# Graph layer with max over seven relations: first batch reordered, row sums turned by VectorE and placed by GpSimd

## The reference

```
h   = relu(layernorm(x))
HW_r = h @ W[r, :128] + c_r          c_r = W_edges[r] @ W[r, 128:]   (one row of 128)
A_0 = A_1 = adj,  A_3 = A_4 = adj^T,  A_2, A_5: a shift over the batch axis or its transpose,  A_6 = identity
out = x + max over r of (A_r @ HW_r) + b
```

## Time and profile before

| | us |
|---|---|
| three runs: median (lowest, highest) | 230.85 (229.27, 233.23) |
| profiled execution: own time | 230.21 |
| its span | 228.5 |
| busy: TensorE / weight loads | 213.9 / 145.1 |
| busy: VectorE | 172.2 |
| busy: ScalarE | 159.0 |
| busy: GpSimd | 57.8 |

### The profile page before, as it was taken

How to read it: one execution, slowest core, us unless ns; L and a number is a source line. 1 busy time by engine, 2 the same in 40 slices (tenths; PEclk the granted TensorE clock), 3 DMA queues, 4 the chain that set the end, 5 groups by cost and what they waited for, 6 DMA issues and landing times.

```text
span 228.5 us, 3306 instructions
## 1 busy us (share of the span) xinstructions
PE 213.9 (94%) x872; PEld 145.1 (63%) x872; DVE 172.2 (75%) x414; ACT 159.0 (70%) x431; POOL 57.8 (25%) x109
## 2 busy tenths in 40 slices
PE   7973799999999899999999999999999998999994
PEld 7532466667676567667667667677666665667672
DVE  3453987697876887897779788797778869787845
ACT  3756928778686777969586877969686867966220
POOL 3106322303232231213223231213223231223200
PEclk9997589999999999999999999999999999999999
DMA  5999907759293955949393866939393966610101
GB/s 184 310 355 371 336 5 243 265 192 303 44 382 103 313 185 200 308 100 331 114 346 127 264 241 209 295 123 348 88 333 123 306 202 238 221 46 3 47 0 46
DMA packets 31586, 47.13 MB, mean 206 GB/s; under 512 B 1632, under 2 KB 11088, under 8 KB 31568
## 3 DMA queue, kind: packets, MB, share of 16 engines
q1 hardware_dynamic: 31568, 46.92, 61.4%
HBM read 42.72 MB, written 4.19 MB: 205 GB/s over the span
## 4 chain that ended last, share of the span: by engine, by line
PE 85%; SPq 5%; DMA 4%; DVE 2%; issue 2%; DVEq 0%
PE bank_g L691 12%; PE bank_p L736 12%; PE bank_gT L673 11%; PE bank_p L738 10%; PE bank_p L737 10%; DMA x_sb<-in_x_dram 4%; PE bank_p L714 3%; PE bank_g L695 3%; PE bank_gT L678 3%; PE bank_gT L679 3%; PE bank_g L696 3%; PE bank_g L699 3%; PE bank_gT L682 3%; PE bank_p L640 3%; PE bank_p L648 3%
## 5 line engine op out<-in xcount | busy, mean ns | idle before, releaser
L548 DVE TENSOR_TENSOR best<-bank_p,best 128x512 f32<-128x512 f32 x48 | 33.2, 692 | 9.1 <-PE bank_p L738 8.1
L295 POOL TENSOR_TENSOR x_bias<-xT_sb,bias_sb 128x512 f32<-128x512 f32 x16 | 20.7, 1294 | 73.7 <-DVE h_lo L517 72.1
L403 ACT ACTIVATE gT_hi<-bank_gT 128x512 fp32r<-128x512 f32 x16 | 9.6, 598 | 37.5 <-PE bank_gT L682 37.1
L691 PE MATMUL bank_g<-adjT_sb,h 128*128 128x512 f32 x60 | 29.0, 605 | 0.0
L545 DVE SCALAR_TENSOR_TENSOR best<-bank_p,c_col,best 128x512 f32<-128x512 f32 x32 | 24.0, 751 | 6.4 <-ACT best L422 5.7
L387 ACT ACTIVATE h<-x_sb,shift,rstd 128x128 f32<-128x128 f32 x60 | 24.7, 491 | 5.9 <-DVE shift L497 5.9
L673 PE MATMUL bank_gT<-adj_sb,h 128*128 128x512 f32 x60 | 28.2, 592 | 0.0
L303 POOL TENSOR_TENSOR o_sb<-best,x_bias 128x512 f32<-128x512 f32 x15 | 19.8, 1320 | 28.2 <-DVE best L548 28.2
L479 DVE BATCH_NORM_STATS2 stats<-x_sb 128x6 f32<-128x128 f32 x64 | 14.0, 281 | 16.4 <-DMA x_sb<-in_x_dram 16.4
L736 PE MATMUL bank_p<-hT_hi,w_hi 128*128 128x512 f32 x48 | 20.1, 419 | 4.0 <-issue 2.9
L511 DVE TENSOR_TENSOR aT_lo<-adjT_sb,aT_hi 128x512 fp32r<-128x512 f32 x30 | 21.8, 767 | 0.0
(11 more groups left out here) (107 smaller groups left out, 470.2 us busy)
## 6 DMA issues: line engine op xcount, KB each, us to landing
adj_sb<-in_adj_dram SPq DMA_DIRECT2D x15, 1024.0 KB, 5.4
adjT_sb<-in_adjT_dram SPq DMA_DIRECT2D x15, 1024.0 KB, 5.8
xT_sb<-in_xT_dram SPq DMA_DIRECT2D x16, 256.0 KB, 6.1
x_sb<-in_x_dram SPq DMA_DIRECT2D x15, 256.0 KB, 6.4
out_dram<-o_sb SPq DMA_DIRECT2D x15, 256.0 KB, 6.0
adj_sb<-in_adj_dram SPq DMA_DIRECT2D x4, 256.0 KB, 3.8
adjT_sb<-in_adjT_dram SPq DMA_DIRECT2D x4, 256.0 KB, 4.4
w_sb<-in_W_dram SPq DMA_DIRECT2D x3, 128.0 KB, 7.0
```

Source lines behind the costliest of these rows:

```text
L295: nc.gpsimd.tensor_tensor(x_bias[q][:, :], xT_sb[q][:, :], bias_sb[:, :], ALU.add).then_inc(xb_ready, 1)
L548: op = nc.vector.tensor_tensor(best[q][:, :], product, best[q][:, :], ALU.max)
L691: nc.tensor.matmul(bank_g[:, 0:N], h[q][:, c, :], adjT_sb[q][:, c, :], start=(c == WHOLE[0]), stop=False)
```

## The change

- x lies in four buffers instead of two (NX = 4); in the loop SyncE issues load_x(b + 3) where load_x(b + 2) stood.
- First loads: the weights of relations 2, 5, 6 and x(1) go out after the first chunk of adjT(0), the other weights ahead of adj(1), and x(2) after adjT(1).
- TensorE's turn_sums and ScalarE's copy_sumsT are gone. sum_parts shrinks to 32 columns for each chunk, of which 8 are used. VectorE turns it in 32x32 blocks (`turned`, row group = node group of 32); GpSimd's `place_sums` spreads it to sumsT of 128 x (4 chunks x 4 groups x 32 nodes), each row group keeping only its own nodes by the mask own_group.
- c_rows gets a plane of 128 rows for each of the four relations, and each c product is one matmul over all 128 rows (`add_sums`). c values come from four matmuls of 128 columns.
- In batch 0 VectorE's list is in another order, w_lo is made in three parts, and TensorE does products 0, 1, then the passes of 3 and 4, product 2, the passes of 5 and 6, and the four c products last (`products_first`).

```diff
@@ sync
-                q = b % 2
-                if b >= 2:
-                    sp.wait_ge(h_ready, b - 1)
+                q = b % NX
+                if b >= NX:
+                    sp.wait_ge(h_ready, b - NX + 1)
...
             for c in range(C):
                 sp.dma_start(adjT_sb[0][:, c, :], adjT_dram[0][:, c, :]).then_inc(adjT0_in[c], 16)
-                if c == 1:
+                if c == 0:
                     sp.dma_start(w_sb[:, 0:1, :], w_dram[:, 2:3, :]).then_inc(wh_in, 16)
                     sp.dma_start(w_sb[:, 1:3, :], w_dram[:, 5:7, :]).then_inc(wh_in, 16)
-            load_x(1)
-            load_adj(1)
+                    load_x(1)
             sp.dma_start(w_sb[:, 3:5, :], w_dram[:, 3:5, :]).then_inc(wa_in, 16)
             sp.dma_start(w_sb[:, 5:7, :], w_dram[:, 0:2, :]).then_inc(wa_in, 16)
+            load_adj(1)
             load_adjT(1)
+            load_x(2)
...
             for b in range(B):
+                if b + 3 < B:
+                    load_x(b + 3)
                 if b + 2 < B:
-                    load_x(b + 2)
                     load_adj(b + 2)
@@ gpsimd
+            def place_sums(b):
+                pool.wait_ge(sumsT_turned, b + 1)
+                if b == 0:
+                    pool.wait_ge(masks_ready, 1)
+                else:
+                    pool.wait_ge(prod_psum, b * NPROD)
+                nc.gpsimd.tensor_tensor(sumsT[:, :, :, :],
+                                        turned[:, :].rearrange("p (c s) -> p c s", c=C).unsqueeze(2)
+                                        .to_broadcast([P, C, C, GROUP]),
+                                        own_group[:, :].unsqueeze(1).unsqueeze(3).to_broadcast([P, C, C, GROUP]),
+                                        ALU.mult).then_inc(sumsT_ready, 1)
...
             part_sums(0)
+            nc.gpsimd.tensor_tensor(w_lo[:, NH + 2:, :], w_sb[:, NH + 2:, :], w_hi[:, NH + 2:, :].bitcast(F32),
+                                    ALU.subtract).then_inc(wlo_ready, 1)
+            place_sums(0)
...
                 part_sums(b)
                 finish(b - 1)
+                place_sums(b)
@@ vector
+            def turn_sums(b):
+                dve.wait_ge(parts_lo, b + 1)
+                if b >= 1:
+                    dve.wait_ge(sumsT_ready, b)
+                nc.vector.transpose(turned[:, :], sum_parts[b % 2][:, :, :].rearrange("p c k -> p (c k)").bitcast(F32)
+                                    ).then_inc(sumsT_turned, 1)
...
             scale_and_shift(1)
+            turn_sums(0)
+            dve.wait_ge(masks_ready, 1)
+            dve.wait_ge(c_step, 2)
+            for d in range(2):
+                rels = slice(2 * d, 2 * d + 2)
+                nc.vector.tensor_scalar(c_low[:, rels, :], c_rest[:, rels, :], row_lo[:, d:d + 1], None,
+                                        ALU.mult).then_inc(c_step, 1)
+                dve.wait_ge(c_step, 3 + d)
+                nc.vector.scalar_tensor_tensor(out=c_rows[:, rels, :], in0=c_hi[:, rels, :].bitcast(F32),
+                                               scalar=row_hi[:, d:d + 1], in1=c_low[:, rels, :], op0=ALU.mult,
+                                               op1=ALU.add).then_inc(crow_ready, 1)
+            split_g_lo(0)
+            take_best(0, 1)
+            split_h_lo(1)
             variance(2)
-            split_g_lo(0)
-            split_h_lo(1)
-            take_best(0, 1)
             take_best(0, 2)
...
                 if b + 1 < B:
                     scale_and_shift(b + 1)
+                turn_sums(b)
+                if b + 1 < B:
                     split_adj_lo(b + 1)
@@ tensor
-                nc.tensor.matmul(to[:, nodes], c_rows[rows, :], sumsT[rows, nodes], start=True, stop=False)
+            def add_sums(i, to, chunks=slice(0, C), start=False, stop=False):
+                return nc.tensor.matmul(to[:, chunks.start * P:chunks.stop * P], c_rows[:, ORDER_A.index(ORDER[i]), :],
+                                        sumsT[:, chunks, :, :].rearrange("k c g s -> k (c g s)"),
+                                        start=start, stop=stop)
+            def products_first():
+
+                product(0, 0)
+                product(0, 1)
+                pe.wait_ge(gTlo_ready, 1)
+                pe.wait_ge(wlo_ready, 2)
+                passes(3, bank_of[3][:, 0:N], start=True)
+                passes(4, bank_of[4][:, 0:N], start=True)
+                pe.wait_ge(ccol_ready, 1)
+                product(0, 2)
+                pe.wait_ge(c_step, 2)
+                pe.wait_ge(wlo_ready, 3)
+                pe.wait_ge(glo_ready, 1)
+                passes(5, bank_of[5][:, 0:N], start=True)
+                passes(6, bank_of[6][:, 0:N], start=True)
+                pe.wait_ge(crow_ready, 2)
+                pe.wait_ge(sumsT_ready, 1)
+                for i in range(NH, NPROD):
+                    add_sums(i, bank_of[i], stop=True).then_inc(prod_psum, 1)
...
             for b in range(1, B):
                 aggregate_T(b)
                 turn_h(b)
-                turn_sums(b)
                 aggregate(b)
```

More of the change, by code:

```diff
@@ L55, in sem @@
             return ctx.enter_context(nc.semaphore(name))
-        x_sb = pair("x_sb", [P, C, F])
+        x_sb = [sb(f"x_sb{i}", [P, C, F]) for i in range(NX)]
         xT_sb = pair("xT_sb", [P, N])
@@ L81, in gnn_kernel @@
         sums = pair("sums", [P, 2, C])
-        sum_parts = pair("sum_parts", [P, C, 2, 2, GROUP], F32R)
-        sumsT = sb("sumsT", [P, N], F32R)
+        sum_parts = pair("sum_parts", [P, C, GROUP], F32R)
+        turned = sb("turned", [P, C * GROUP])
+        sumsT = sb("sumsT", [P, C, C, GROUP], F32R)
         x_bias = pair("x_bias", [P, N])
@@ L106, in gnn_kernel @@
         e_blocks = sb("e_blocks", [R * REL, R])
-        e_rows = sb("e_rows", [R * REL, 4, GROUP])
+        e_rows = sb("e_rows", [R * REL, 4, P])
         bias_sb = sb("bias_sb", [P, N])
         c_col = sb("c_col", [P, R])
[L110 to L115, removed]
+        row_hi = sb("row_hi", [P, 2])
+        row_lo = sb("row_lo", [P, 2])
+        own_group = sb("own_group", [P, C])
+        c_hi = sb("c_hi", [P, 4, O], F32R)
+        c_rest = sb("c_rest", [P, 4, O])
+        c_low = sb("c_low", [P, 4, O])
+        c_rows = sb("c_rows", [P, 4, O], F32R)
         bank_gT = bank("bank_gT")
@@ L126, in gnn_kernel @@
         x0_in = [sem(f"x0_in{i}") for i in range(2)]
-        x_in = [sem(f"x_in{i}") for i in range(2)]
+        x_in = [sem(f"x_in{i}") for i in range(NX)]
         xT_in = [sem(f"xT_in{i}") for i in range(2)]
@@ L192, in times, with x_loads @@
             return 16 * ((b + 1) // 2)
+        def x_loads(b):
+            return 16 * (b // NX + int(b % NX > 0))
         def turns(b):
@@ L317, in _ @@
             for q in range(2):
-                last = nc.gpsimd.memset(sum_parts[q][:, :, :, :, :].bitcast(F32), 0.0)
+                last = nc.gpsimd.memset(sum_parts[q][:, :, :].bitcast(F32), 0.0)
             last.then_inc(parts_zeroed, 1)
@@ L448, in _ @@
             make_h(1)
-            copy_sumsT(0)
             act.wait_ge(ccol_ready, 1)
@@ L459, in _ @@
                 split_hT(b)
-                copy_sumsT(b)
                 if b + 1 < B:
@@ L477, in variance @@
                     elif b > 0 and c == 0:
-                        dve.wait_ge(x_in[q], times(b))
-                    last = nc.vector.bn_stats(stats[:, c, :], x_sb[q][:, c, :])
+                        dve.wait_ge(x_in[b % NX], x_loads(b))
+                    last = nc.vector.bn_stats(stats[:, c, :], x_sb[b % NX][:, c, :])
                 last.then_inc(stats_done, 1)
@@ L578, in _ @@
             dve.wait_ge(c_psum, 1)
-            nc.vector.tensor_copy(c_col[:, :], bank_c[:, 0:R]).then_inc(ccol_ready, 1)
-            nc.vector.tensor_copy(c_hi[:, :], bank_c[:, P:2 * P]).then_inc(c_step, 1)
+            c_psum_rows = bank_c[:, :].rearrange("p (r o) -> p r o", r=4)
+            nc.vector.tensor_copy(c_col[:, :], bank_ccol[:, 0:R]).then_inc(ccol_ready, 1)
+            nc.vector.tensor_copy(c_hi[:, :, :], c_psum_rows).then_inc(c_step, 1)
             dve.wait_ge(c_step, 1)
-            nc.vector.tensor_tensor(c_rest[:, :], bank_c[:, P:2 * P], c_hi[:, :].bitcast(F32),
+            nc.vector.tensor_tensor(c_rest[:, :, :], c_psum_rows, c_hi[:, :, :].bitcast(F32),
                                     ALU.subtract).then_inc(c_step, 1)
[L584 to L589, removed]
             variance(1)
@@ L641, in turn_h @@
                 last.then_inc(hT_psum, 1)
[L643 to L651, removed]
             def aggregate_T_first():
@@ L735, in product @@
                     hi, lo = g_hi, g_lo
-                nc.tensor.matmul(dst, w_hi[:, i, :], hi[:, nodes], start=(r in H_RELS), stop=False)
+                nc.tensor.matmul(dst, w_hi[:, i, :], hi[:, nodes], start=start, stop=False)
                 nc.tensor.matmul(dst, w_lo[:, i, :], hi[:, nodes], start=False, stop=False)
```

(27 more changed lines are left out.)

57 lines of the change are left out of this document (21 added, 36 removed).

## The result

| | median us (lowest, highest) | runs |
|---|---|---|
| before, beside it | 230.21 (229.27, 233.23) | 4 |
| after | 234.51 (233.64, 235.89) | 4 |

The ratio is 1.021, interval 1.013 to 1.028: the changed kernel is slower, but since 1.02 lies inside the interval, the runs do not settle whether it is slower by as much as 2%. The ratio leaves out the 233.23 of before, an execution in a slower state (1.7% above the fastest), and so differs a little from the quotient of the medians, 1.019. The profiled execution of the changed kernel took 235.89, its span 234.2; it is the slowest of its four.

The account below looks back on a forecast made before the run. TensorE bounds the kernel before; after the change VectorE's late hT_lo stalls it every batch. Batch 2 at 41.4, twelve batches of 13.65, batch 14 of 13.34 and a 16.5 tail give span 235.0, time 237; range 226 to 245.

Parts of the forecast that it names:

- The mechanism: VectorE's a_lo pair: GpSimd's placement runs between the two subtractions, delays hT_lo, and TensorE stalls in every batch.
- the hold: Blocking of VectorE's second a_lo subtraction by GpSimd's placement: +1.09 us a batch, bounds below 0 to above 2.6.
- period: Time per batch: hT_lo at +7.46, wanted at +6.64, product 0 at +7.56, plus 6.09: 13.65 us against a mean of 12.91.
- The c products: TensorE, each batch: four full passes at 0.234, 0.94, replace 0.62 of row-group passes and slower return: +0.31 us.
- The start: Up to batch 2: batch 1 begins 5.4 to 7.4 us earlier, about 2 survive; batch 2 at 41.4, before 43.46.
- a fall of the granted clock in the stalls: TensorE's clock could fall in stalls of 1 us; given nothing beyond the upper end of the range.
- Batch 14 and the tail: Batch 14, full collision without variance: 13.34 us; batch 15 and the tail, no stall: 16.5 against 16.86.
- The hidden placement: First rival: GpSimd served after both a_lo, beneath gT_lo and hT_lo; TensorE bounds at 12.47, time 220.6; chance 0.18.
- the second rival: Part of the hold hidden by shorter placement or escaping aT_lo pair: 0.3 to 0.8 off a period, 226 to 233; chance 0.15.
- The third: GpSimd slower on broadcast operands: 1.6 us instead of 1.28 gives 241.5, twice the time 255; chance 0.07.
- The x waits: VectorE's waits for x go with four buffers: up to -4.1 us; the rival that they stay shares the 0.07.

Follow-up runs that it names:

- The moved line: The changed kernel with VectorE's turn_sums after the two a_lo subtractions instead of before them: 221.66 us, ratio 0.966.
- the quarter: The changed kernel with GpSimd placing only one chunk of four from batch 1 on: one run of 224.14 us.
- the memset: The changed kernel with GpSimd's placement replaced from batch 1 on by a memset of the same tile: one run of 222.84 us.
- hT_lo first: The changed kernel with VectorE's list reordered: turn the sums, gT_lo, hT_lo, then the a_lo pair; 219.39 us, ratio 0.955.
- variance(3) late: The kernel with hT_lo ahead of the a_lo pair, and in batch 1 variance(3) after g_lo: 219.68 us, ratio 0.956.

## Why the prediction was right

It said 237 with the step slower, from a profiled execution of 236.7; the profiled one took 235.89 and the median is 234.51. Against the kernel before that is a loss of 4.3 us where 6.2 were forecast (237 for 230.85). The range of 226 to 245 would have held no change at all as well, so what the prediction is worth shows in its terms.

- **The mechanism held.** GpSimd got its turn between the two a_lo subtractions, TensorE was ready at +6.64 as counted, and TensorE stalled in every batch up to batch 14. The moved line, the quarter and the memset show that the hold, and not the work added, makes the loss.
- **The hold was sized too large:** 1.09 counted, 0.82 measured. The sum took over the hold that the o_sb addition makes, a GpSimd pass of 1.28 by itself; the placement, with both operands broadcast, takes 1.04 by itself. From the start of the transpose to the next instruction it is 0.23 (0.2 counted). hT_lo at +7.21 for +7.46, period 13.37 in the batch shown for 13.65; the twelve batches from 43.38 to 204.26 average 13.41, 2.9 us less than forecast in all.
- **The c products** came at +0.30 for +0.31. TensorEngine Tiling (Array Packing) in the Trainium skill (key properties) says that different tiles run in parallel, and also that a change of tiling mode drains TensorE. The prediction set only the first against the full passes; the rows fit both: four 32-row passes took 0.43 together, and the first full pass behind them 0.42 instead of 0.23.
- **The start** was right up to 28.2: batch 1 began at 23.45 in the timeline (23.4), the last maximum of batch 0 ended at 28.21 (28.6), and TensorE waited for it. Then one term failed: the prediction gave a fall of the granted clock in the stalls nothing beyond the upper end of the range, and counted all of batch 1 at full clock. TensorE stood 1.21 and 2.91 us, and its next passes ran at half clock. Timeline of TensorE after, and the stretch with its granted clock (columns as in the earlier trace rows):

```profile
34.60 0.76 PE L752 MATMUL bank_p<-hT_hi,w_hi 128*128 128x512 f32 x1 [2.91 <-issue]
35.17 0.63 PE L753 MATMUL bank_p<-hT_hi,w_lo 128*128 128x512 f32 x1
...
34.60:40.30 5.70, 5.70 (x14) 4.44 (x15) 2.34 (x4) 4.04 (x13) 1.99 (x5) 0.50 0.61 207
```

  Batch 2 began at 43.38 instead of 41.4. From product 0 on, 34.60 to 43.38 is 8.78 where a full clock needs 6.05: 2.7 us. Of the 7.2 gained in batch 0 (23.45 for 30.68 in the timelines) nothing was left. How much of this the other executions pay is not shown: their mean granted clock was 0.985 to 0.993 against 0.980 in the profiled one, and their spans were 1.4 to 2.3 us shorter.
- **Batch 14 and the tail.** Batch 14 took 13.07 for 13.34. The tail was to shrink by 0.37 and took 16.87, as before: the maxima began 0.38 earlier in it, and VectorE then waited 0.58 before the last one, where it had waited 0.20. Why is not shown. The full-height c passes are not the cause: put on the kernel before, they leave that wait at 0.20.
- **The errors offset, by luck:** -2.9 in the twelve batches and -0.3 in batch 14 against +2.0 at batch 2 and +0.4 in the tail leave the span at 234.2 for 235.0. A good total is not evidence for its terms.
- **The rivals.** The hidden placement was priced at 220.6; the moved line gave 221.66 and hT_lo first 219.39, so the price was about right and the order decides. A part of the second rival came true, the shorter placement: it takes 0.28 off the period, where that rival began at 0.3. The third had the sign wrong, since the pass with broadcast operands is shorter (1.04) and not longer than one with dense operands (1.28). The x waits went, as forecast. They were priced at the 4.1 of the long batches, 4.2 measured, but four x buffers are worth 6.4 on the kernel before, with their 2.45 at the start.

## What to carry to other kernels

Before work moves to an engine that has time to spare, look at what its neighbour runs at the moment it will start: here a GpSimd pass of 1.04 us with both operands in SBUF, on an engine 33% busy, cost VectorE 0.82 in each batch because it started beside two subtractions that read two SBUF tensors; behind them, beneath passes that read PSUM, it held nothing up. When an added step brings an engine's list within a few tenths of where another waits for it, first put the result that is waited for ahead of those that are not: hT_lo before a_lo was worth 2.3 us more than the moved line. And test the parts of a change alone, since one part may be paying for another.

## What the runs showed of the hardware

- A near miss costs more than its size: with the quarter of the placement a TensorE wait of 0.05 us before product 0 went with a batch of 12.75, against 12.46 with hT_lo first and no wait. The 0.29 are the wait and the first pass behind it, which takes 0.47 instead of 0.23.
- A GpSimd pass that reads SBUF and becomes ready inside the first of two subtractions with two SBUF inputs runs before the second, which waits for it: passes of 0.40, 1.04 and 1.28 added 0.18, 0.82 and 1.09 to the pair.
- The granted clock is not told by one stall. In the kernel with hT_lo first it stayed 1.00 after waits of 1.78 us and, 4 us later, 0.87. In the one with variance(3) late, 1.93 us of waiting was followed by a stretch at 0.65. In the one with the moved line, after waits of 0.70 and 2.06, TensorE worked for 1.4 us at 0.99 and then for 3.1 us at 0.50 (34.00 to 37.10).
